# Cross-attention, 20 heads, two layers: the products that turn the row maxima go behind score fill 9 instead of ahead of it

## The reference

```
q, k, v  = heads(x @ Wq), heads(text @ Wk), heads(text @ Wv)
out_text = softmax(q k^T / sqrt(8)) v                    # 1593 tokens in layer 0, 1597 in layer 1
layer 0: out_ip = softmax(q k_ip^T / sqrt(8) + mask) v_ip # the last 8 tokens
layer 1: the weights of out_ip also need qsem = probs @ text (256 channels per head), its norm, its dot products
x        = (out_text + out_ip) @ Wout + b + x
```

## Time and profile before

| what | us |
|---|---|
| time, median of 3 runs (1613.88 to 1620.68) | 1617.58 |
| the profiled execution's own time | 1620.16 |
| its span (first to last instruction) | 1617.9 |
| PE busy | 1459.4 (90%) |
| DVE busy | 1146.8 (71%) |
| ACT busy | 1066.6 (66%) |
| POOL busy | 179.4 (11%) |
| attention steps of layer 0 | about 205 to 617 |
| attention steps of layer 1 | about 673 to 1570 |

### The profile page before, as it was taken

The page is one execution under the profiler, slowest core; times in us unless marked ns, Lnnn a source line. Parts: engine busy times, 40 slices in busy tenths (PEclk is TensorE's granted clock), DMA queues, the critical chain, the costliest instruction groups (busy, mean ns, idle before and its releaser), DMA issues. The chain is left out here.

```text
span 1617.9 us, 37267 instructions
## 1 busy us (share of the span) xinstructions
PE 1459.4 (90%) x12870; PEld 904.4 (56%) x12870; DVE 1146.8 (71%) x1679; ACT 1066.6 (66%) x1892; POOL 179.4 (11%) x328
## 2 busy tenths in 40 slices
PE   6799778888888888589999999999999999999995
PEld 4455412222222225257777776767677676767774
DVE  4888777777777762677767677767677676767725
ACT  2465457777777783177777776767677676767752
POOL 3643300000000001100000000000000000000000
PEclk9899869999999998779999999999999999999996
DMA  5267741111111110310111110011101111001000
GB/s 147 84 184 209 190 114 48 47 47 47 47 47 47 47 32 18 88 35 23 26 27 28 29 26 21 25 29 28 29 18 25 29 28 29 23 21 32 6 1 16
DMA packets 79631, 80.93 MB, mean 50 GB/s; under 512 B 28248, under 2 KB 66764, under 8 KB 79516
## 3 DMA queue, kind: packets, MB, share of 16 engines
q1 hardware_dynamic: 79516, 79.20, 18.4%
HBM read 50.39 MB, written 28.75 MB: 49 GB/s over the span
## 5 line engine op out<-in xcount | busy, mean ns | idle before, releaser
L1160 DVE TENSOR_TENSOR pl<-pe,ph 128x1024 f16<-128x1024 f32 (+1 forms) x280 | 319.6, 1142 | 96.4 <-ACT ph L1092 94.1
L1089 ACT ACTIVATE pe<-ps_x 128x1024 f32<-128x1024 f32 x240 | 246.2, 1026 | 133.6 <-PE ps_x L979 128.7
L1145 DVE TENSOR_REDUCE mx<-ps_y 128x2 f32<-128x800 f32 (+2 forms) x240 | 236.1, 984 | 123.0 <-PE ps_y L931 123.0
L1015 PE MATMUL ps_v<-eh,ph 128*128 128x269 f16 x1040 | 292.6, 281 | 0.0
L1015 PE MATMUL ps_n<-eh,ph 128*128 128x269 f16 x1040 | 290.6, 279 | 0.0
L1092 ACT CAST ph<-pe 128x1024 f16<-128x1024 f32 (+1 forms) x280 | 275.6, 984 | 8.9
L1018 PE MATMUL ps_v<-eh,pl 128*128 128x269 f16 x960 | 268.4, 280 | 3.7 <-issue 3.7
L1017 PE MATMUL ps_v<-el,ph 128*128 128x269 f16 x960 | 269.5, 281 | 0.0
L1017 PE MATMUL ps_n<-el,ph 128*128 128x269 f16 x960 | 268.0, 279 | 0.0
L1018 PE MATMUL ps_n<-eh,pl 128*128 128x269 f16 x960 | 266.9, 278 | 0.0
L1145 DVE TENSOR_REDUCE mx<-ps_x 128x2 f32<-128x800 f32 x160 | 158.6, 991 | 115.4 <-PE ps_x L931 115.3
(11 more groups left out here) (314 smaller groups left out, 1889.1 us busy)
## 6 DMA issues: line engine op xcount, KB each, us to landing
v_cols<-vcut SPq DMA_DIRECT2D x4, 1690.0 KB, 13.5
vb<-v_cols SPq DMA_DIRECT2D x40, 169.0 KB, 2.3
e<-in_ctx SPq DMA_DIRECT2D x4, 1536.0 KB
kb<-k_parts SPq DMA_DIRECT2D x80, 74.9 KB
kb<-k_parts SPq DMA_DIRECT2D x80, 74.7 KB
k_parts<-kp SPq DMA_DIRECT2D x12, 400.0 KB
vb<-v_cols SPq DMA_DIRECT2D x40, 117.0 KB, 2.0
qb<-q_parts SPq DMA_DIRECT2D x160, 25.0 KB
```

The source lines that it names most:

```text
L1015: pe.matmul(ps, hi, eh, start=(t == 0), stop=False)
L1089: nc.scalar.activation(dst, src, ACT.Exp, scale=SCALE).then_inc(exp_done, 1)
L1145: nc.vector.tensor_reduce(mx[:, (o + d) % 2, c, :], scores_bank(p)[:, :, 0:w], AX.X, ALU.max).then_inc(chunk_max, 1)
L1160: nc.vector.tensor_tensor(pl[:, o % 2, t0:t1, :], pe32[:, 0, t0:t1, :], ph[:, o % 2, t0:t1, :], ALU.subtract).then_inc(low_done, 1)
```

## The change

`turn_max` is issued when p is 10, not 9: behind score fill 9 and just ahead of exponent fill 10. No instruction and no wait is added or removed.

```
                 def step(k, o):
                     for p in range(FILLS):
-                        if p == 9:
+                        if p == 10:
                             turn_max(k, o)
                         if p in EXP_AT:
                             exponents(k, o, p)
```

## The result

The changed kernel takes 1604.73 us (median of 6 runs, 1601.3 to 1608.17); the kernel before, run beside it, 1620.51 us (6 runs, 1613.88 to 1623.14). The ratio is 0.990 with a 95% interval of 0.9878 to 0.9921: 1% faster, about 16 us. The forecast was 16.8 us.

The account below looks back on a forecast made before the run. Layer 0 was taken as bound by a chain between engines (max 7, turn, fill 9, max 9, fills 12 and 13), layer 1 by PE's queue. -18.5 - 2.0 + 3.7 = -16.8 us gave 1600.8 us, range 1595 to 1609.

Parts of the forecast that it names:

- Layer 0, 0.50 us a step, 18.5 us: Layer 0, steps 1 to 37: fill 9 no longer stands behind the turn's wait for max 7; saves 37 x 0.50 us.
- PE's own order at fill 12: Layer 0: PE reaches fill 12 0.18 us behind fill 11, 0.50 us earlier than before, no longer waiting for max 9.
- the thin cover of ACT at fill 13: Layer 0: exponential e5 is released at 415.12, only 0.08 us before PE's order brings fill 13.
- Layer 1, +3.7 us: Layer 1: one more seam from fill to full-depth work, 0.10 us in 37 steps; bounds 0 and 7.4 us.
- The reading of the seam from fill 10's two lengths: Fill 10 takes 0.11 us before a fill, 0.21 before 128-row products; so a seam costs about 0.10 us.
- the rival with free seams: Layer 1: the turn slips in behind fill 9 without loss; layer 1 even, -20.5 us, 1597.1 us; chance 0.20.
- a second seam hidden in the turn's 0.21 us: Layer 1: upper bound of the seam price, 0.20 us instead of the 0.10 taken.
- First steps, 2.0 us: First step with a turn of each layer: DVE's idle before max 9 closes, 1.0 us each; bounds 0 and 2.6.
- The sum: Whole kernel: -18.5 - 2.0 + 3.7 = -16.8 us, from 1617.58 to 1600.8 us.

Follow-up runs that it names:

- e3: Against the kernel before, the turn goes ahead of fill 11 instead of fill 9 in both layers; 1623.54 us, ratio 0.9996 to before.
- e4: Against the changed kernel, layer 1 issues the turn in two halves by head, behind fills 9 and 10; 1620.95 us, ratio 0.9978 to before.
- e5: Against the changed kernel, layer 1's turn is in two halves, each with one product per head, behind fills 9 and 10; 1615.79 us (1 run).
- e10: Against the changed kernel, layer 1 is written out without a loop; 1581.49 us, ratio 0.9764 to before.
- e2: Against the kernel before, the turn goes behind fill 9 in layer 1 only; 1624.20 us, ratio 1.0011 to before.
- e6: Against the kernel before, same order, but layer 0's turned maxima go into a free bank, ps_n; 1604.54 us, ratio 0.9887 to before.
- e8: Against the kernel before, turn behind fill 9 in layer 0 only and layer 1 written out without a loop; 1582.16 us, ratio 0.9749 to before.

## Why the prediction was right, point by point

**Layer 0, 0.50 us a step, 18.5 us.** Right in mechanism and size. Fill 9, max 9, the turn, fill 12 and fill 13 stand within 0.02 us of where the working put them, counted from fill 7. The lead over before grows by 0.50 us in each of 37 steps; at the last turn of layer 0 it is 20.86 us, at the third, where the steady pattern begins, 2.38. What was called next in line, PE's own order at fill 12 and the thin cover of ACT at fill 13, was so too: 0.06 us against the 0.08 of the working; e3 used it up.

**Layer 1, +3.7 us.** Right: 0.105 us a step. The reading of the seam from fill 10's two lengths gave the right price. The rule of the Trainium skill named in the prediction (page "TensorEngine Tiling (Array Packing)", section "Key Properties"), that a change of tiling mode drains TensorE, spoke for the forecast and against the rival with free seams. The trace agrees: the one change more costs 0.10 us. The count of changes agrees as well: before, units, turn, fills, units has three (the last unit starts at 1003.68 and takes 0.115, the turn starts at 1003.88, so 0.09 us lie there too), after, units, fill, turn, fills, units has four. What the working took as open, a second seam hidden in the turn's 0.21 us, is what e4 and e5 point to, but it was there before too and so cancels. The expectation of e4 counted neither that seam (0.10 us) nor that a half turn of one head is as long as a whole one (0.11 us), and missed by 0.21 us.

**First steps, 2.0 us.** This is the term that was mis-sized: the idle time of DVE before max 9 goes as forecast, but little of it reaches the time. In layer 0 the second turn comes 8.29 us behind the first instead of 9.11, a gain of 0.82 us that every kernel with the turn behind fill 9 repeats (8.29 or 8.30), against the forecast 1.0. The next step gives 0.12 of it back (11.35 us instead of 11.23). Its length goes with the granted clock, which comes back from half 17.8 us behind the first turn in the one trace and 17.9 in the other: in other kernels with the new order it is 10.71 us where the clock is back after 16.4 us (e5) and 11.82 where it is after 19.5 (e4). Where the clock is back after 17.5 us in both orders, the new one again takes 0.11 us more (e10 11.14, e2 11.03). So the term is 0.7 us in layer 0. At the third turn the lead is 2.38 us, but 1.68 of that was there at the first turn already and is not of the change's making: 0.88 comes from the stage before, and 0.79 from fill 7 ahead of the first turn, which waits for its queries to be loaded and waited longer in this execution of the kernel before. First the kernel before, then the changed one:

```profile
211.18 0.51 PE L931 MATMUL ps_y<-kb,qb 50*128 50x400 bf16 x2 [1.56 <-DMA qb<-q_parts]
...
209.34 0.52 PE L931 MATMUL ps_y<-kb,qb 50*128 50x400 bf16 x2 [0.61 <-DMA qb<-q_parts]
```

In layer 1 I counted 1.0 and got 0.15. Max 9 does run back to back there:

```profile
659.30 0.98 DVE L1145 TENSOR_REDUCE mx<-ps_x 128x2 f32<-128x800 f32 x1
```

and the second turn of layer 1 is 0.9 us nearer to the first (12.15 instead of 13.04 us). But the step after that is 0.75 longer (21.52 instead of 20.77). The granted clock is at half at that time, and its units came earlier while the clock did not: the units took 0.225 us each until 705.2 in the one trace, 3.3 us behind their start, and until 682.8 in the other, 4.2 us behind it. The four more slow units account for some 0.4 us of the 0.75; the rest is open. Other runs bear this out. The same two steps are 12.15 and 21.59 us in e2 and 12.15 and 21.73 in e10, so the gain is lost again each time. And in e6, which has the order of before in layer 1, the clock came back 25.1 us behind the first turn instead of about 23.4, and there this step takes 21.62 us with the old order too.

**The sum.** The effects of the code by the steps are 18.5 + 0.7 in layer 0 (first turn to third), and in layer 1 + 0.15 for the first two steps and - 3.6 for the rest (36 x 0.105, less 0.17 in the last, which has no fill 9): 15.75 us. The medians differ by 15.8, the forecast was 16.8; the 1 us between is the first steps, 2.0 in the forecast and 0.85 here. The profiled spans differ by 19.5 us, because in this pair of executions other stages happened to be shorter as well: 1.7 us ahead of the first turn, 1.5 between the layers and 0.7 at the loop ends of layer 1. The absolute time was 3.9 us above the forecast, of which 2.9 are that before itself was measured at 1620.51 and not at 1617.58; its runs scatter by 9 us, so it is in part luck that the 1.0 us left fits what the first steps fell short by.

**The stall of layer 1.** The working took PE in layer 1 to be busy throughout and never asked about the other 9.9 of 400 us. It made no difference to the change, but 23 us were lying there.

## What to carry to other kernels

In a queue worked in order, an instruction's wait is paid by all that stands behind it: look for the work that is ready but queued behind a wait that it doesn't need, and put it ahead, or take away what the other waits for (e6 did as well as the move). Before moving, follow the next link of the chain to see how far the gain goes (here 0.50 of the 0.65 us that DVE had been idle) and which path has the least cover left. And check the stage that did not wait: there the same move can only cost, so choose the order by stage where the code allows it.

## What the runs showed of the hardware

- TensorE loses about 0.10 us at a change between products over 50 rows in both halves of the array and products over all 128 rows. From a fill to full-depth products it is read directly (fill 10: 0.11 us before a fill, 0.21 before products). In the other direction it is 0.10 us behind units (982.68 to 982.89, where a unit's product alone takes 0.115), 0.12 behind products with v (0.55 against 0.43 us), and an estimated 0.10 behind the turn (e4, e5). From full-depth products of 128 columns to those of 2 it loses 0.09 us (units to turn, before); from 9 columns to 2 it loses nothing (0.43 us from the start of one block to the next in e6). A short full-depth block between fills thus costs 0.20 us plus its own time.
- Small products that write different halves of the partitions stream side by side, if they are issued next to each other: two of one head take 0.05 us more than one of each head (0.21 and 0.15 us with the seam, e4 and e5).
- The end of a loop over a long body cost PE 2.2 to 3.8 us in layer 1 (steps of 23.8 to 25.4 us instead of 21.6), differently each time. In layer 0, where a step has about half as many PE instructions (some 410 products in four steps against some 800), the steps at the loop's end are 10.00 us like the others, and no instruction packets come in from 280 to 600 us. In layer 1 they do all the time, in a burst at each loop end, and PE goes on 1.6 to 1.8 us after the end of such a packet. Written out, layer 1 ran without any of it, 23 us faster. The page's rows of the instruction queues change with it:

```profile
q8 instruction: 96, 1.57, 0.4%
q14 instruction: 19, 0.16, 0.0%
```

before (kind: packets, MB, share), and in e8:

```profile
q8 instruction: 74, 1.21, 0.3%
q14 instruction: 34, 0.28, 0.1%
```
